# Attention and FFN phase of a post-norm decoder layer: in the chunks that also carry an out-projection, the first FFN units are placed between the blocks of scores, and the second chunk's x1 is loaded and summed earlier

## What is computed

```python
x = _layernorm(x + _L0_attn_ref(x, ...))
x = _layernorm(x + _L0_xattn_ref(x, ctx_1024, ctx_1024, ..., mask_1x1xSxS2_ik0))
x = _layernorm(x + _L0_ffn_ref(x, ...))
```

```python
hidden = jnp.einsum('bsd,df->bsf', x, W1) + b1
imag = w_imag * jnp.sin(theta + hidden * 0.1)
q = hidden + (jnp.cos(theta) * w_real + jnp.sin(theta) * w_imag) * imag * 0.1
return jnp.einsum('bsf,fd->bsd', jax.nn.relu(q), W2) + b2
```

## Time and profile before

| | |
|---|---|
| median of 3 runs | 3189.76 us |
| lowest, highest | 3187.53, 3192.28 us |
| profiled execution, its own time | 3192.79 us |
| its span from first to last instruction | 3191.1 us |
| mean granted TensorE clock | 0.958 of 2.4 GHz |
| TensorE busy with matmuls | 2836.6 us |
| VectorE, ScalarE, GpSimd busy | 2687.3, 2016.4, 1836.3 us |

### The profile page before, as it was taken

How to read it: one execution, slowest core, us unless ns; L and a number is a source line. 1 busy time by engine, 2 the same in 40 slices (tenths; PEclk the granted TensorE clock), 3 DMA queues, 4 the chain that set the end, 5 groups by cost and what they waited for, 6 DMA issues and landing times. The chain is left out here.

```text
span 3191.1 us, 48817 instructions
## 1 busy us (share of the span) xinstructions
PE 2836.6 (89%) x18964; PEld 1271.5 (40%) x18964; DVE 2687.3 (84%) x3064; ACT 2016.4 (63%) x3618; POOL 1836.3 (58%) x949
## 2 busy tenths in 40 slices
PE   5888988978988988988978889889999999999998
PEld 2222222222222222222222222556666676667765
DVE  3899999999999999999999988666666677777775
ACT  4676776776766766676676745555555555555564
POOL 3698987887887987988988898221111211112100
PEclk8999999999999999999999989899999999999999
DMA  4111111111111111112112143701111000001000
GB/s 154 44 45 55 47 57 43 47 57 44 57 50 50 47 50 60 50 37 65 45 44 83 40 131 125 233 14 48 47 45 41 29 29 22 22 24 34 29 8 14
DMA packets 120118, 172.77 MB, mean 54 GB/s; under 512 B 13265, under 2 KB 48721, under 8 KB 119378
## 3 DMA queue, kind: packets, MB, share of 16 engines
q1 hardware_dynamic: 119890, 169.63, 16.5%
HBM read 100.92 MB, written 66.58 MB: 52 GB/s over the span
## 5 line engine op out<-in xcount | busy, mean ns | idle before, releaser
L790 POOL TENSOR_TENSOR h<-h,c_rep 128x1024 f32<-128x1024 f32 x511 | 1197.2, 2357 | 274.6 <-ACT carry L572 273.8
L719 DVE TENSOR_TENSOR_SCAN h<-r_ps,carry,h 128x512 f32<-128x512 f32 x768 | 938.9, 1262 | 8.8 <-ACT r_ps L566 8.5
L566 ACT ACTIVATE r_ps<-r_ps,decay 128x512 f32<-128x512 f32 x1024 | 632.0, 656 | 357.0 <-PE r_ps L340 356.7
L706 DVE TENSOR_TENSOR h<-u_ps,b_rep 128x1024 f32<-128x1024 f32 x512 | 614.4, 1200 | 64.8 <-PE u_ps L351 63.1
L351 PE MATMUL u_ps<-dtu,spread 32*128 32x512 f16 x2048 | 320.5, 391 | 104.2 <-DVE h L706 103.6
L340 PE MATMUL r_ps<-dt,spread 32*128 32x512 f16 x2048 | 314.7, 387 | 57.4 <-DVE h L719 44.7
L367 PE MATMUL y_ps<-h,gather 128*32 128x512 f32 x2048 | 287.0, 628 | 57.4 <-POOL h L790 54.5
L1824 POOL TENSOR_TENSOR o_in<-o_in,rows 128x1024 f32<-128x1024 f32 x15 | 35.9, 2395 | 510.2 <-DMA o_in<-o_dram 510.2
L719 DVE TENSOR_TENSOR_SCAN h<-r_ps,zero,h 128x512 f32<-128x512 f32 x256 | 313.1, 1264 | 7.9 <-ACT r_ps L566 7.8
L40 PE MATMUL fps<-x,region 128*128 128x256 f16 x1024 | 284.1, 277 | 3.5 <-issue 2.4
L41 PE MATMUL fps<-x,region 128*128 128x256 f16 x1024 | 283.5, 277 | 0.0
(11 more groups left out here) (247 smaller groups left out, 5732.1 us busy)
## 6 DMA issues: line engine op xcount, KB each, us to landing
u_t_dram<-u SPq DMA_DIRECT2D x16, 1024.0 KB, 4.8
z_t_dram<-zs SPq DMA_DIRECT2D x32, 512.0 KB, 3.0
uz<-u_t_dram SPq DMA_DIRECT2D x64, 256.0 KB, 3.9
uz<-z_t_dram SPq DMA_DIRECT2D x64, 256.0 KB, 4.3
y_t_dram<-y SPq DMA_DIRECT2D x64, 256.0 KB, 2.4
region<-y_t_dram SPq DMA_DIRECT2D x32, 256.0 KB, 3.6
result<-x SPq DMA_DIRECT2D x16, 512.0 KB, 2.8
x_t<-dram_x_t SPq DMA_DIRECT2D x15, 512.0 KB, 4.0
```

What stands on the lines that cost most here:

```text
L566: nc.scalar.activation(bank, bank, ACT.Exp, scale=decay[:, col:col + 1]).then_inc(s_da, 1)
L706: nc.vector.tensor_tensor(h[:, g % H_GROUPS, o:o + 2, :], u_ps[:, :, :], b_rep[:, c % 2:c % 2 + 1, :].broadcast_to([P, 2, TS]), ALU.mult). ...
L719: nc.vector.tensor_tensor_scan(row, r_ps[:, 2 * (pair % 2) + o, :], row, start, ALU.mult, ALU.add)\
L790: nc.gpsimd.tensor_tensor(rows, rows, c_rep[:, c % 2:c % 2 + 1, :].broadcast_to([P, 2, TS]), ALU.mult)\
```

## The change

In the bodies with an out-projection (1 to 6) each engine's list is ordered anew. On PE `hidden` 2 and 3 and `second` 0 and 1 go between the blocks of scores. On ACT the two copies of the out-projection go between sines and relus of units 0 and 1. On DVE the fractions, mixes and low parts of units 0 and 1 go ahead of the first scores. For chunk 2 alone, SP loads o_in and x in `first()`, POOL adds o_in's bias there, ahead of one of y's low parts, and x's sum and y's low part of the body's second tile come ahead of x2's bias. ACT makes that tile's high part behind the last weight pieces, and DVE takes x1's statistics after two fractions. The lists of bodies 7 to 16 stay.

```diff
@@ sync, first()
                 load_piece(7)
+                sp.wait_ge(s_x1, 1)
+                load(o_in[:, :, :], chunk_rows("o", 2), s_oin)
                 store_projection(1, o_out[:, :])
...
                 load_piece(9)
+                sp.wait_ge(s_rwo, NT)
+                load(x1[:, 0, :, :], chunk_rows("x", 2), s_xin)
@@ sync, body
-                if more:
+                if more and late:
                     sp.wait_ge(s_rwo, c * NT)
                     load(x1[:, 1 - par, :, :], chunk_rows("x", c + 1), s_xin)
@@ tensor, body, with ops
                         out_projection(c, m * NT, sps)
                         out_projection(c, m * NT + 1, sps)
+                    hidden(b, 2)
                     scores(c, 0, batch, (0, 1), ops)
+                    hidden(b, 3)
+                    scores(c, 0, batch, (2, 3), ops)
+                    second(b, 0)
+                    scores(c, 1, batch, (0, 1), ops)
+                    hidden(b, 4)
+                    scores(c, 1, batch, (2, 3), ops)
+                    second(b, 1)
...
-                if front:
-                    scores(c, 0, batch, (2, 3), ops)
-                hidden(b, 2)
-                if front:
-                    scores(c, 1, batch, (0, 1), ops)
-                hidden(b, 3)
-                if front:
-                    scores(c, 1, batch, (2, 3), ops)
-                second(b, 0)
-                hidden(b, 4)
-                second(b, 1)
@@ scalar, body
                 if not late:
-                    y_high(Y_PAIRED - 1)
                     weights_high(8)
                     weights_high(9)
-                if more:
+                    y_high(Y_PAIRED - 1)
+                elif more:
                     deviation("x1", 0, c + 2)
...
                 for m in ops:
+                    if not late:
+                        deviation("x1", 0, c + 2)
+                    sine(b, 0)
                     out_evacuated(m * NT, sps)
+                    sine(b, 1)
+                    relu(b, 0)
+                    relu(b, 1)
                     out_evacuated(m * NT + 1, sps)
-                sine(b, 0)
-                hid_out(b, 2)
-                relu(b, 0)
-                sine(b, 1)
-                hid_out(b, 3)
-                relu(b, 1)
-                sine(b, 2)
-                relu(b, 2)
-                if front:
+                    hid_out(b, 2)
+                    sine(b, 2)
+                    hid_out(b, 3)
+                    sine(b, 3)
+                    relu(b, 2)
+                    relu(b, 3)
                     exps(c, 0)
                     exps(c, 1)
+                    hid_out(b, 4)
@@ vector, body
-                if more:
+                if more and late:
                     statistics("x1", 0, c + 1, x1[:, 1 - par, :, :])
...
+                if ops:
+                    fraction(b, 0)
+                    fraction(b, 1)
+                    if not late:
+                        statistics("x1", 0, c + 1, x1[:, 1 - par, :, :])
+                        normalize("x1", 0, c + 1, x1[:, 1 - par, :, :])
+                    mix(b, 0)
+                    mix(b, 1)
+                    act_low(b, 0)
+                    act_low(b, 1)
                     masked(c, 0, (0, 1))
+                    fraction(b, 2)
                     masked(c, 0, (2, 3))
+                    row_maximum(c, 0)
+                    mix(b, 2)
+                    fraction(b, 3)
                     masked(c, 1, (0, 1))
+                    less_maximum(c, 0)
+                    mix(b, 3)
+                    act_low(b, 2)
                     masked(c, 1, (2, 3))
                     row_maximum(c, 1)
+                    act_low(b, 3)
                     less_maximum(c, 1)
+                    fraction(b, 4)
@@ gpsimd, first() and body
-                for i in range(1, Y_PAIRED - 1):
+                for i in range(1, Y_PAIRED - 2):
                     y_low(i)
+                o_bias(2)
+                y_low(Y_PAIRED - 2)
...
-                if more:
+                if more and late:
                     pool.wait_ge(s_avl, c * NT)
                     o_bias(c + 1)
...
                     x1_sum(c + 1, 1 - par)
+                if not late:
+                    for m in ops:
+                        y_low(m * NT + 1)
                 x2_bias(c - 1, 1 - par)
-                for m in ops:
-                    y_low(m * NT + 1)
+                if late:
+                    for m in ops:
+                        y_low(m * NT + 1)
```

More of the change, by code:

```diff
@@ L1298, in body @@
                     hidden(b, 1)
-                if front:
-                    scores(c, 0, batch, (2, 3), ops)
-                hidden(b, 2)
-                if front:
-                    scores(c, 1, batch, (0, 1), ops)
-                hidden(b, 3)
-                if front:
-                    scores(c, 1, batch, (2, 3), ops)
-                second(b, 0)
-                hidden(b, 4)
-                second(b, 1)
+                    if front:
+                        scores(c, 0, batch, (2, 3), ())
+                    hidden(b, 2)
+                    if front:
+                        scores(c, 1, batch, (0, 1), ())
+                    hidden(b, 3)
+                    if front:
+                        scores(c, 1, batch, (2, 3), ())
+                    second(b, 0)
+                    hidden(b, 4)
+                    second(b, 1)
                 hidden(b, 5)
@@ L1515, in body @@
                 for m in ops:
+                    if not late:
+                        deviation("x1", 0, c + 2)
+                    sine(b, 0)
                     out_evacuated(m * NT, sps)
+                    sine(b, 1)
+                    relu(b, 0)
+                    relu(b, 1)
                     out_evacuated(m * NT + 1, sps)
-                sine(b, 0)
-                hid_out(b, 2)
-                relu(b, 0)
-                sine(b, 1)
-                hid_out(b, 3)
-                relu(b, 1)
-                sine(b, 2)
-                relu(b, 2)
-                if front:
+                    hid_out(b, 2)
[4 more added lines that the diff above has]
+                    relu(b, 3)
                     exps(c, 0)
                     exps(c, 1)
-                sine(b, 3)
-                hid_out(b, 4)
-                relu(b, 3)
+                    hid_out(b, 4)
+                if not ops:
+                    sine(b, 0)
+                    hid_out(b, 2)
+                    relu(b, 0)
+                    sine(b, 1)
+                    hid_out(b, 3)
+                    relu(b, 1)
+                    sine(b, 2)
+                    relu(b, 2)
+                    if front:
+                        exps(c, 0)
+                        exps(c, 1)
+                    sine(b, 3)
+                    hid_out(b, 4)
+                    relu(b, 3)
                 sine(b, 4)
@@ L1755, in body @@
                     normalize("w2", 2, d, x2[:, par, :, :])
-                if more:
-                    normalize("x1", 0, c + 1, x1[:, 1 - par, :, :])
-                if front:
+                    if more:
+                        normalize("x1", 0, c + 1, x1[:, 1 - par, :, :])
[4 more added lines that the diff above has]
+                        statistics("x1", 0, c + 1, x1[:, 1 - par, :, :])
+                        normalize("x1", 0, c + 1, x1[:, 1 - par, :, :])
+                    mix(b, 0)
+                    mix(b, 1)
+                    act_low(b, 0)
+                    act_low(b, 1)
@@ L1759, in body @@
                     masked(c, 0, (0, 1))
-                fraction(b, 0)
-                if front:
+                    fraction(b, 2)
                     masked(c, 0, (2, 3))
-                fraction(b, 1)
-                mix(b, 0)
-                if front:
+                    row_maximum(c, 0)
+                    mix(b, 2)
+                    fraction(b, 3)
                     masked(c, 1, (0, 1))
-                    row_maximum(c, 0)
-                fraction(b, 2)
-                act_low(b, 0)
@@ L1770, in body @@
-                mix(b, 1)
-                if front:
-                    masked(c, 1, (2, 3))
[L1773 to L1777, removed]
+                    less_maximum(c, 0)
+                    mix(b, 3)
+                    act_low(b, 2)
+                    masked(c, 1, (2, 3))
                     row_maximum(c, 1)
-                act_low(b, 2)
-                if front:
+                    act_low(b, 3)
@@ L1781, in body @@
                     less_maximum(c, 1)
-                mix(b, 3)
-                fraction(b, 4)
-                act_low(b, 3)
+                    fraction(b, 4)
+                else:
+                    if front:
+                        masked(c, 0, (0, 1))
+                    fraction(b, 0)
+                    if front:
+                        masked(c, 0, (2, 3))
+                    fraction(b, 1)
+                    mix(b, 0)
+                    if front:
```

(19 more changed lines are left out.)

## The result

| | before | changed |
|---|---|---|
| median | 3188.98 us (4 runs) | 3168.24 us (4 runs) |
| lowest, highest | 3187.53, 3192.28 | 3164.88, 3169.16 |
| profiled execution, its span | 3192.79, 3191.1 | 3168.42, 3166.7 |

A forecast was written before the change was run, and what follows sets the result against it. TensorE was busy 89% of the span, so time is won only where it waits or runs at its lower clock. 18.0 us (chunks 2 to 6) plus 5.0 (chunk 1) make 23.0: 3167 us against a 3189.8 median, range 3158 to 3175.

The forecast's parts named there:

- 3.6 us a chunk, 18.0 for five: Chunks 2 to 6: excess of 3.8 us between out-projection and second 0 goes, less 0.2 for switches.
- The 0.2 for more switches between kinds of matmul: PE in chunks 2 to 6: 0.2 us taken off each chunk's gain for two more switches, which stay.
- 5.0 us: Chunk 1's net gain: 13.0 us of gains less losses of 2.3, 1.4, 2.9 and 1.4; bounds 1 and 13.0.
- the forecast's sign: Chunk 1: the queries start later than 2068.01 by 2 to 4 us; a start at 2068 would prove it wrong.
- + 1.4: Chunk 1: low-clock loss of 1.4 us behind each of two PE waits, at the queries and the first scores.
- (b): Chunk 1: y's low part ends in time, but x2's bias delays DVE's mask; PE waits 2.9 us, plus 1.4 low clock.
- Zero, at most +1: SP's queue: o_in's early load ahead of a projection store costs nothing, as ACT has 2 us of slack; at most 1 us.
- No collision reaching PE: Rival for chunk 1: POOL's operations delay no DVE work that PE needs; 31 us saved, 3159 us; chance 0.2.
- Low clock staying in chunks 2 to 6: Rival: each chunk keeps 1.3 us of low clock and 0.8 of wait, gaining 1.5; 3177 us; chance 0.17.
- No change, by giving back at the chunk's end: Rival: PE's gain in mid-chunk is lost at its end to DMA and POOL; about 3188 us; chance 0.05.
- Slower by a late copy: Rival: second tile's copy on ACT exceeds its 2.0 us margin, each further us lost in six chunks; chance 0.03.
- The lock: DVE and POOL: one waits for the other's whole instruction, so a small DVE operation took 2.06 us.

The follow-up runs named there:

- e1: Changed kernel with the new order kept in chunks 2 to 6 alone, chunk 1 and early loads taken back; 3170.2 us, 0.9925 of the kernel before.
- e5: Changed kernel with POOL's o_in addition for chunk 2, and x1's bias and sum, moved behind DVE's normalization of x2; 3164.9 us, run once.
- e7: Changed kernel with the edits of e5 and e6, and x1's statistics ahead of the first fraction; 3158.4 us, 0.9900 of the kernel before.
- e6: Changed kernel with DVE's chunk 1 mask ahead of the last two weight pieces, POOL's x2 bias behind chunk 1's first values; 3161.4 us, run once.
- e4: Changed kernel with the second tile's copy put behind hid_out 2 on ACT in chunks 2 to 6; 3190.5 us, run once.
- e9: e7 with o_in's load for chunk 2 behind the second out-projection tile's store on SP instead of ahead; 3155.6 us, run once.

## Why the prediction was right, and where it was off

**Chunks 2 to 6, "3.6 us a chunk, 18.0 for five".** Right in mechanism and 2.0 us low. Each gave 4.0 (e1 shows it alone). Two terms were missing. The wait of `hidden` 6 for `hid_out` 4, left at zero, went as well: `second` 2 to `hidden` 6 is now 2.59 us instead of 2.83. And the excess was counted from the end of the last out-projection matmul, 2255.28 + 0.38, where the next one of its kind would have cost 0.22: 0.16 too little. The 0.2 for more switches between kinds of matmul was right. In the kernel before, `second` 0 took 2.59 us and `hidden` 4 2.62:

```profile
2271.70 0.27 PE L40 MATMUL fps<-x,region 128*128 128x256 f16 x1
...
2274.32 0.38 PE L40 MATMUL nat<-region,act 128*128 128x512 f16 x1
```

With scores behind them they take 2257.04 - 2254.34 = 2.70 and 2260.81 - 2258.09 = 2.72. So 3.8 + 0.16 - 0.2 + 0.24 is the 4.0 that was measured. I read chunk 3 for all five. Chunk 5 was 1.6 longer and chunk 6 1.6 shorter, which cancelled by luck.

**Chunk 1, "5.0 us".** It gave 2.9. The waits were near the forecast: L1756 and its successor took 2.1 us more (2.29 + 2.05 against 2.06 + 0.17; 2.3 forecast) and the normalization 1.15 more (1.0 forecast), which made 3.2 us of wait at the x2 transposes, then 2.6 ahead of the first scores where 2.9 was worked out. The queries' first matmul was 0.8 us later than the old one in span time, where the forecast's sign asked for 2 to 4, and 2.5 later against chunk 1's start (2.3 forecast). Span time was the wrong scale for that sign, since the start itself moves by more from trace to trace.

The term that failed is "+ 1.4", twice, for the low clock: it cost 2.8 and 3.3, together 3.3 us more than forecast. Other terms took 1.2 of that back: against 72.4 us of work the old losses without the queries' own waits were 13.4, not 13.0, and the waits now sum to 5.8 where 3.7 + 2.9 was implied. I had taken `hidden` 2 of chunk 3 as the price of any low stretch. The trace of before held other prices, in chunks 5 and 6, had I looked beyond one chunk.

**Cancelling.** 2.0 too little in one part and 2.1 too much in the other made 23.0 of 22.9 us. The total was that near by luck; the two parts were good to 2 us each. It is near in the traces alone, and counted in medians the kernel gained 20.7 us where 22.8 was forecast.

**(b), y's low part ready in time:** yes, PE's list shows no wait for it. **SP's queue, "Zero, at most +1":** ACT waited for the store about 1 us longer (1.37 us, 0.31 before). That was hidden behind POOL's collisions in the changed kernel, and came out as 1.1 to 1.3 us of wait at the x2 transposes once e5 and e7 removed those. So the bound was about right; the reason given for zero (slack of ACT) held only as long as DVE was later still.

**Rivals.** No collision reaching PE: fallen, both did (e5, e6). Low clock staying in chunks 2 to 6: fallen, 1.00. No change, by giving back at the chunk's end: fallen, chunks 7 and 8 take 65.08 and 65.25 us (65.03 and 65.25 before). Slower by a late copy: its price per us was set too low. e4 lost 4.0 us for 2.3 of lateness, but in chunks 2 to 6 the copy had about 2 us to spare, as forecast, and the rival did not occur.

**The lock.** The prediction leaned on the Trainium skill ("SBUF — State Buffer", "Who interferes with whom"). By its rule the runs agree. In e5 the same two small operations take 0.17 us each while POOL is idle, and a later one of that kind takes 2.06 beside y's low part. The last two weight pieces take 4.49 us where POOL's operation has to wait for them, and 6.41 in e5 where one of POOL's falls between them. L1609, which reads PSUM, takes 1.22 us beside a POOL operation in e5 and 1.21 without one in the changed kernel.

## What to carry to other kernels

Read a wait of TensorE together with the stretch behind it, and over all repetitions of the loop rather than one: the same two waits came with 0, 1.6 or 3.2 us of low clock. Put a job between every two uses of a PSUM bank that another engine must read in between, on all engines' lists at once; moving the job on PE alone only moved the wait. And when GpSimd work is moved earlier, look up which VectorE operations it will stand beside: a bias addition that was issued earlier put POOL beside two VectorE operations of 16 elements a partition instead of one, and each took 2 us instead of 0.17.

## What was not expected of the hardware

The granted clock behind equal waits differed. Behind waits of 0.78 and 1.01 us `hidden` 2 took 2.72 us in chunk 6, 3.98 in chunk 3 and 5.23 in chunk 5, in one trace. Single waits of 2.30 (e4), 2.58 and 3.21 us (changed) cost a further 1.7, 3.3 and 2.8, and one of 4.53 us (e5) no more than 2.8; waits of up to 1.42 us (e7) cost nothing beyond themselves. So the price did not follow the length of the wait. What decides between the cases was not tested, and stays open. Also, a 256 KB store landed 5.7 us after its issue in e7, where a 512 KB load was issued ahead of it, and 4.1 us after it in e9, where the load came behind. ACT waited 1.25 us for it in e7 and not at all in e9.
